# Block 0's two output products in the attention loop: issued whole behind a half-step's scores, or in two column halves around the next step

## The chip, the cores and the metric

One core of one Trainium2 chip runs the kernel. The metric is the device time of one execution in microseconds: 515.57 us before the change, the median of 3 runs (515.53 to 515.69).

## The reference

A layer with post-normalisation on x of 2 x 1024 rows of 512: attention with 8 heads of width 8, then a gated feed-forward part with int4 weights and group scales (1792 wide), each with a residual and a layer norm. Cut to what matters here:

```python
qk = (x @ Wqk_w.T + Wqk_b).reshape(b, n, H, E, 2)          # H = E = 8
v = (x @ Wv_w.T + Wv_b).reshape(b, n, H, E)
scores = jnp.einsum('bhqd,bhkd->bhqk', q, k)
attn = jax.nn.softmax(scores, axis=-1) / 8
out = jnp.einsum('bhsl,bhlv->bhsv', attn, v)               # -> (b, n, 64)
attention = out @ Wo_w.T + Wo_b                            # 64 -> 512
x = layernorm(x + attention)
x = layernorm(x + (silu(x @ Wg.T) * (x @ Wu.T)) @ Wd.T)    # Wg, Wu, Wd dequantised
```

The change touches `out @ Wo_w.T` of the first 512 rows only.

## The kernel before

The 2048 rows are cut into four blocks of 512 queries (NB = 4), and the eight heads into two groups of four. The attention loop has ALL = 64 steps `n`: block by block, group by group, and within a group the eight tiles of 128 keys. A step has two half-steps (`pair` 0 and 1), each with two heads. Steps 0 to 15 are block 0, steps 16 to 31 block 1.

All of it is Bass code in which each engine's program is written out by hand, with semaphores. Per half-step the engines do this:

- TensorE writes the scores of two heads (L1087, two matmuls of 512 columns that share the array by rows), a pair of first-pass matmuls (L1012), and half of the weighted sums of the step before (L1116, `av`, four heads side by side in 256 of the 512 columns).
- ScalarE takes the exponential of both heads' scores in one instruction of 1024 elements (L782, `exps`).
- VectorE takes row maxima of the first pass (L1315), one instruction a matmul. The first pass computes the scores once more ahead of time, so that the maxima of a group of heads are there before the group starts: 256 matmuls (FIRST), two each half-step, into a ring of three banks (RING). TensorE may write a ring bank when the reduction three places earlier is done.

Between these come "turns", which `turns_at(n, pair)` places in the second half-steps: `M`, the transposed maxima of a coming group; `avT` and `attT`, transposes of a group's and of a block's attention; and `wo`, the output product. For block 0, `WO_AT = (3, 4)` puts its two products into steps 19 and 20; blocks 1 and 2 have theirs in the last steps with banks of their own, block 3 behind the loop. A product (in `turn`, L1063) takes 128 columns of `attT` for each of two row tiles and writes two banks of 512 columns, in float32. ScalarE copies both to `wob` (`wo_out`, L810), and GpSimd adds them to x later (L641).

Scores and turns share four PSUM banks in two pairs, in the order in which `in_shared_banks` lists them, each use taking the other pair than the one before. So a use must wait for the use two places earlier to be read:

```python
for n in range(ALL):
    for pair in range(2):
        order += [("scores", n, pair)] + turns_at(n, pair)
...
if pi >= 2:
    wait_shared_read(pe, *shared[shared_index["scores", n, pair] - 2])
```

Around the first product the list reads scores (19,0), scores (19,1), product 0, scores (20,0), scores (20,1), product 1, scores (21,0), and so on: scores (20,0) wait for the exponential of scores (19,1), and scores (20,1) for the copy of product 0. In a step behind a turn (`firsts_ahead`) the first-pass pair of half-step 0 comes ahead of the scores; in all others it comes behind them. TensorE's program for one half-step is the loop behind `for n in range(DRAIN)`, ScalarE's the one around `exps(n, pair)`.

Of the kernel before, what the change touches and what calls it, by code (L numbers as in the profile page):

```python
# [21 lines left out]
P = 128  # L22
# [3 lines left out]
HD = H * E  # L26
# [3 lines left out]
TB = 512  # L30
# [27 lines left out]
def build(nc, x, xT, wqkT, bqk, wvT, bv, woT, bo, gq, gs, uq, us, dq, ds, ds_next, spread, out):  # L58
    ctx = ExitStack()
    with ctx:  # L60
# [42 lines left out]
        wo_s = sb("wo_s", [2 * HD, D], F32)  # L103
# [168 lines left out]
        def turns_at(n, pair):  # L272

            if pair == 0:
                return []
            f, r = divmod(n + 3, KT)
            if r == 0 and f < NB * NG:
                return [("M", f, 0)]
            f, r = divmod(n - 9, KT)
            if r == 0 and 0 <= f < LASTF:  # L280
                return [("avT", f, 0)]
            r = n - STEPS
            if r == 2:
                return [("attT", 0, 0)]
            if r in WO_AT:
                return [("wo", 0, WO_AT.index(r))]
            return []
# [47 lines left out]
        def shared_banks(*use):  # L335
            return 2 * ((shared_index[use] + 1) % 2)

        def wait_shared_read(engine, kind, n, k):

            if kind == "scores":  # L340
                engine.wait_ge(s_exp, 2 * n + k + 1)
            elif kind == "avT":
                engine.wait_ge(s_norm, n + 1)
            else:
                engine.wait_ge(s_read, out_count[kind, n, k])
# [381 lines left out]
        def _(act):  # L727
# [46 lines left out]
            def exps(n, pair):  # L774

                pi, at = 2 * n + pair, shared_banks("scores", n, pair)
                act.wait_ge(s_scf, pi + 1)
                if pi == 0:
                    act.wait_ge(s_row, 5)
                if n >= 2 and pair == 0:  # L780
                    act.wait_ge(s_av, 2 * (n - 1))
                nc.scalar.activation(pbuf[:, pi % 4, :].rearrange("p (a n) -> p a n", a=2), ps[:, at:at + 2, :], ACT.Exp,  # L782
                                     scale=gamma[:, n // (ALL // B):n // (ALL // B) + 1]).then_inc(s_exp, 1)
# [32 lines left out]
            def turn_out(kind, u, k):  # L816
                if kind == "attT":
                    att_out(u)
                if kind == "wo":
                    wo_out(u, k)  # L820
                if kind == "M":
                    max_out(u)
# [24 lines left out]
            for n in range(ALL):  # L847
                for pair in range(2):
                    exps(n, pair)
                    if pair and n and n % KT == 0:  # L850
                        av_out(n // KT - 1)
                    for use in turns_at(n, pair):
                        turn_out(*use)
            nc.scalar.activation(warm[:], mhalf[:, 0:1], ACT.Silu)
            av_out(NB * NG - 1)

# [77 lines left out]
        def _(pe):  # L934
# [85 lines left out]
            def ring_use(kind, n):  # L1020
                i = ring_index[kind, n]
                if i >= 3:

                    wait_ring_read(pe, *ring_order[i - 3])
                if kind == "first":
                    first_pass(n)
                elif kind == "tops":
                    turn_tops(n, ring_bank(kind, n))
                else:
                    turn_maxima(0, ring_bank("M", 0)).then_inc(s_rf, 1)  # L1030

            def turn(kind, u, k):

                if (kind, u, k) in aside:
                    wait_ring_read(pe, "first", FIRST - 1)
                    for other in before_in_bank(kind, u, k):
                        wait_aside_read(pe, other)
                    at = aside_bank(kind, u, k)
                else:
                    i = shared_index[kind, u, k]  # L1040
                    wait_shared_read(pe, *shared[i - 2])
                    at = shared_banks(kind, u, k)
                dst = bank[at]
                if kind == "M":
                    mm = turn_maxima(u, dst)
                elif kind == "avT":

                    pe.wait_ge(s_ave, u + 1)
                    for t in range(BT):
                        mm = nc.tensor.transpose(dst[:, t * P:(t + 1) * P], avt[:, u % 2, t * P:(t + 1) * P], ident[:])  # L1050
                elif kind == "attT":

                    pe.wait_ge(s_norm, NG * (u + 1))
                    for t in range(0, BT, 2):
                        mm = nc.tensor.transpose(dst[:, t * HD:(t + 2) * HD],
                                                 att[:, u, t:t + 2, :].rearrange("p t n -> p (t n)"), ident[:])
                else:
                    if k == 0:
                        pe.wait_ge(s_wo, 16)
                        wait_attT(pe, u)  # L1060
                    for j in range(2):
                        rows = slice(j * HD, (j + 1) * HD)
                        mm = nc.tensor.matmul(bank[at + j], attT[rows, k * P:(k + 1) * P], wo_s[rows, :],  # L1063
                                              start=True, stop=True)
                mm.then_inc(s_of, 1)

            def scores(n, pair):

                u, s = divmod(n, STEPS)
                g, kt = divmod(s, KT)  # L1070
                b, k = divmod(u, N // TB)
                pi = 2 * n + pair
                if kt == 0 and pair == 0:
                    pe.wait_ge(s_mld[g], 16 * 2 * (u + 1))
                at = shared_banks("scores", n, pair)
                if pi >= 2:
                    wait_shared_read(pe, *shared[shared_index["scores", n, pair] - 2])
                elif pi == 0:

                    pe.wait_ge(s_vc, 2 * B)  # L1080
                    pe.wait_ge(s_kept, len(placed) - 1)
                    pe.wait_ge(s_kept1, 1)
                else:
                    pe.wait_ge(s_projr, 6)
                for j in range(2):
                    rows, t = slice(ROWS * j, ROWS * (j + 1)), 2 * g + pair
                    mm = nc.tensor.matmul(bank[at + j], ks[b][rows, t, kt * P:(kt + 1) * P],  # L1087
                                          qs[b][rows, k, t, :], start=True, stop=True)
                mm.then_inc(s_scf, 1)
# [14 lines left out]
            def av(n, half):  # L1104

                u, s = divmod(n, STEPS)
                g, kt = divmod(s, KT)
                b = u * TB // N
                pe.wait_ge(s_exp, 2 * n + 2)
                if n == 0:  # L1110
                    pe.wait_ge(s_vc, 2 * B)
                if kt == 0 and n:
                    pe.wait_ge(s_ave, n // KT)
                lo, hi = half * TB // 2, (half + 1) * TB // 2
                for j in range(HG):
                    mm = nc.tensor.matmul(bank[AVB][j * VC:(j + 1) * VC, lo:hi], vst[b][:, kt, g * HG + j, :],  # L1116
                                          pbuf[:, (2 * n + j // 2) % 4, (j % 2) * TB + lo:(j % 2) * TB + hi],
                                          start=(kt == 0 and half == 0), stop=(kt == KT - 1), skip_group_check=True)
                mm.then_inc(s_av, 1)
# [48 lines left out]
            for n in range(DRAIN):  # L1168
                after_group_start = n % KT == 1
                for pair in range(2):  # L1170
                    firsts_ahead = n and pair == 0 and turns_at(n - 1, 1)
                    if firsts_ahead:
                        for use in ring_uses_at(n, pair):
                            ring_use(*use)
                    scores(n, pair)
                    if after_group_start and pair:
                        av(n - 1, 0)
                    if not firsts_ahead:
                        for use in ring_uses_at(n, pair):
                            ring_use(*use)  # L1180
                    for use in turns_at(n, pair):
                        turn(*use)
                    if n and (pair or not after_group_start):
                        av(n - 1, pair)
            for n in range(DRAIN, ALL):
                scores(n, 0)
                for use in aside_at(n, 1):
                    turn(*use)
                scores(n, 1)
                for use in turns_at(n, 1):  # L1190
                    turn(*use)
                av_whole(n - 1)
# [405 lines left out]
```

## Time and profile before

| | |
|---|---|
| median of 3 runs | 515.57 us |
| the profiled execution | 515.66 us |
| its span, first to last instruction | 513.8 us |
| granted TensorE clock, mean | 0.999 |
| busy, TensorE / VectorE / ScalarE / GpSimd | 499.6 / 410.4 / 405.4 / 258.4 us |
| exponentials, L782 | 128, mean 1114 ns |
| first-pass reductions, L1315 | 256, mean 682 ns |
| copies of products to `wob`, L810 | 4, of 1.02 us |

The profiled execution took 1.9 us more than its span, which is counted from the first to the last instruction. Busy times of TensorE are those of overlapping matmuls: two rows that start 0.23 us apart may each last 0.38 us. Where an instruction group "x4" stands in a row, its time runs from the start of the first to the end of the last. The attention loop of this section ends near 212 us, and the products of block 0 stand at 100.60 and 104.05 us.

### The profile page before, as it was taken

What the parts mean: (1) busy time and instruction counts of PE and PEld (TensorE: products, weight loads), DVE (VectorE), ACT (ScalarE), POOL (GpSimd) and SP (SyncE); (2) the same over time, 40 slices, a digit from 0 to 9 for tenths busy, and PEclk for the clock granted to TensorE, in tenths of its full rate; (3) what the DMA queues carried; (4) which work ended last, traced back from release to release, by engine and by line L of the source; (5) the groups of instructions that cost most, each with busy time, mean ns of one, the idle gap of its engine ahead of it and who ended that gap; (6) DMA issues with size and microseconds to landing.
All of it is one profiled execution on the core that took longest, in us unless ns stands there. A gap on an engine that the chain in (4) does not pass through costs nothing.

```text
span 513.8 us, 8129 instructions
## 1 busy us (share of the span) xinstructions
PE 499.6 (97%) x2986; PEld 194.5 (38%) x2986; DVE 410.4 (80%) x699; ACT 405.4 (79%) x563; POOL 258.4 (50%) x298
## 2 busy tenths in 40 slices
PE   8999999999999999999999999999999999999994
PEld 3222233323333322334444444444444444444441
DVE  2799999999999996478778778778668666788676
ACT  1523889898898889868888888888888888888883
POOL 9200091833101624072664686676885874748741
PEclk9999999999999999999999999999999999999999
DMA  6410017675720007600041121130020020000022
GB/s 194 149 57 13 14 50 206 196 144 108 112 40 2 2 5 142 247 1 0 4 59 20 22 41 22 20 63 1 1 82 1 0 84 0 3 0 1 0 82 82
DMA packets 30151, 29.21 MB, mean 57 GB/s; under 512 B 19488, under 2 KB 21920, under 8 KB 29856
## 3 DMA queue, kind: packets, MB, share of 16 engines
q1 hardware_dynamic: 26544, 22.41, 15.5%
q0 software_dynamic: 3424, 6.03, 6.5%
q8 instruction: 23, 0.38, 0.3%
q10 hardware_dynamic: 144, 0.26, 0.1%
q14 instruction: 16, 0.13, 0.1%
HBM read 24.37 MB, written 4.23 MB: 56 GB/s over the span
## 4 chain that ended last, share of the span: by engine, by line
PE 87%; DVE 7%; ACT 3%; issue 1%; DMA 1%; SPq 0%; POOLq 0%; POOL 0%; DVEq 0%
PE ps L1139 19%; PE ps L1127 19%; PE ps L1218 18%; PE ps L1116 9%; PE ps L1012 7%; PE ps L1087 6%; DVE mxh L1315 4%; PE ps L942 3%; ACT pbuf L782 3%; PE ps L1063 1%; PE ps L1099 1%; DMA arena<-xT 1%; PE ps L994 1%; PE ps L952 1%; PE ps L1050 1%
## 5 line engine op out<-in xcount | busy, mean ns | idle before, releaser
L1315 DVE TENSOR_REDUCE mxh<-ps 128x1 f32<-128x512 f32 x256 | 156.7, 682 | 3.3 <-PE ps L1012 2.4
L782 ACT ACTIVATE pbuf<-ps,gamma 128x1024 f32<-128x1024 f32 x128 | 137.2, 1114 | 16.6 <-PE ps L1087 13.1
L865 ACT ACTIVATE ps<-ps,ratio 128x512 f32<-128x512 f32 x167 | 105.8, 659 | 41.5 <-PE ps L1127 38.6
L1218 PE MATMUL ps<-wd,stack 128*128 128x512 f16 x440 | 129.7, 379 | 0.0
L1139 PE MATMUL ps<-arena,wu 128*128 128x512 f16 x448 | 115.4, 379 | 0.0
L1127 PE MATMUL ps<-arena,wg 128*128 128x512 f16 x448 | 115.3, 379 | 0.1
L1499 DVE TENSOR_TENSOR ps<-ps,stack 128x512 f32<-128x512 f32 x128 | 87.8, 695 | 32.3 <-PE ps L1218 30.3
L871 ACT ACTIVATE ps<-ps,ratio 128x512 f32<-128x512 f32 x156 | 98.9, 659 | 5.6 <-PE ps L1139 1.2
L1499 DVE TENSOR_TENSOR ps<-ps,pbuf 128x512 f32<-128x512 f32 x76 | 52.6, 696 | 23.2 <-PE ps L1218 22.4
L677 POOL CAST stack<-pbuf 128x512 f16<-128x512 f32 x55 | 33.5, 609 | 74.5 <-DVE pbuf L1474 74.5
L1116 PE MATMUL ps<-pbuf,arena 128*32 128x256 f32 x832 | 66.5, 391 | 0.4
L679 POOL TENSOR_TENSOR stack<-pbuf,stack 128x512 f16<-128x512 f32 x55 | 63.6, 1156 | 4.5
L1127 PEld LDWEIGHTS ps<-arena,wg 128*128 128x128 f16 x448 | 43.5, 98 | 54.4 <-issue 1.7
L1139 PEld LDWEIGHTS ps<-arena,wu 128*128 128x128 f16 x448 | 43.4, 98 | 54.2 <-DVE pbuf L1474 2.7
L1218 PEld LDWEIGHTS ps<-wd,stack 128*128 128x128 f16 x440 | 43.0, 98 | 52.1 <-DVE ps L1499 0.4
L1012 PE MATMUL ps<-stack 64*128 64x512 f16 x256 | 61.1, 383 | 1.3 <-DVE mxh L1315 0.7
L1087 PE MATMUL ps<-stack 64*128 64x512 f16 x256 | 50.5, 385 | 0.8 <-ACT pbuf L782 0.5
L573 POOL CAST mp<-mx 128x16 f16<-128x16 f32 x8 | 1.6, 196 | 98.0 <-DVE mx L1325 98.0
L1474 DVE SCALAR_TENSOR_TENSOR pbuf<-ps,scales,pbuf 128x512 f32<-128x512 f32 x56 | 41.9, 748 | 6.3 <-PE ps L1139 6.1
L879 ACT ACTIVATE pbuf<-ps,scales 128x512 f32<-128x512 f32 x56 | 38.1, 680 | 0.2 <-PE ps L1127 0.2
L1012 PEld LDWEIGHTS ps<-stack 64*128 64x128 f16 x256 | 21.1, 93 | 41.5 <-DVE mxh L1315 34.8
L1087 PEld LDWEIGHTS ps<-stack 64*128 64x128 f16 x256 | 12.3, 93 | 47.9 <-issue 30.9
(126 smaller groups left out, 389.4 us busy)
## 6 DMA issues: line engine op xcount, KB each, us to landing
arena<-xT SPq DMA_DIRECT2D x16, 256.0 KB, 5.8
x<-x SPq DMA_DIRECT2D x2, 2048.0 KB, 9.8
out<-x SPq DMA_DIRECT2D x3, 1024.0 KB, 4.2
stack<-down_ratios SPq DMA_DIRECT2D x1, 2048.0 KB, 9.6
wg<-gq POOLq DMA_DIRECT2D x4, 448.0 KB, 7.3
wu<-uq POOLq DMA_DIRECT2D x4, 448.0 KB, 7.2
wd<-dq POOLq DMA_DIRECT2D x2, 896.0 KB, 10.7
pbuf<-down_ratios SPq DMA_DIRECT2D x1, 1536.0 KB, 6.3
```

The costliest lines, as they stand in the source:

```text
L679: nc.gpsimd.tensor_tensor(mparts[:, 1, t % NM, :], sg[t % 2], mparts[:, 0, t % NM, :], ALU.subtract)\
L782: nc.scalar.activation(pbuf[:, pi % 4, :].rearrange("p (a n) -> p a n", a=2), ps[:, at:at + 2, :], ACT.Exp, scale=gamma[:, n // (ALL // B) ...
L865: nc.scalar.activation(gbank[t % 2], gbank[t % 2], ACT.Copy, scale=gr[:, t % G, c:c + 1])\
L871: nc.scalar.activation(ubank[t % 2], ubank[t % 2], ACT.Copy, scale=ur[:, t % G, c:c + 1])\
L1012: nc.tensor.matmul(ring_bank("first", n), qs[b][rows, k, t, qt * P:(qt + 1) * P], ks[b][rows, t, half * TB:(half + 1) * TB], start=True, s ...
L1087: mm = nc.tensor.matmul(bank[at + j], ks[b][rows, t, kt * P:(kt + 1) * P], qs[b][rows, k, t, :], start=True, stop=True)
L1116: mm = nc.tensor.matmul(bank[AVB][j * VC:(j + 1) * VC, lo:hi], vst[b][:, kt, g * HG + j, :], pbuf[:, (2 * n + j // 2) % 4, (j % 2) * TB + ...
L1127: mm = nc.tensor.matmul(gbank[t % 2], wg[:, c, i * P:(i + 1) * P], x1v[blk][:, a, c, :, :], start=(c == 0 and a == 0), stop=(a == 1), skip ...
L1139: mm = nc.tensor.matmul(ubank[t % 2], wu[:, c, i * P:(i + 1) * P], x1v[blk][:, a, c, :, :], start=(c == 0 and a == 0), stop=(a == 1), skip ...
L1218: mm = nc.tensor.matmul(bank[k], mparts[:, a, t % NM, k * P:(k + 1) * P], wd[:, i, :], start=(i == 0 and a == 0), stop=(a == 1), skip_grou ...
L1315: nc.vector.tensor_reduce(mxh[:, f % 2, qh, half:half + 1], ring_bank("first", n), AX.X, ALU.max)\
L1499: nc.vector.tensor_tensor(dst, bank[k], by, ALU.mult).then_inc(s_dr[k], 1)
```

## The change

TensorE: a product of block 0 is no longer a turn in its half-step. `begin_product` computes columns 0 to 255 of both banks behind the half-step's weighted sums; `finish_product` computes columns 256 to 511 in the next step, behind the scores of its half-step 0, and signals the whole product. ScalarE: the copy to `wob` comes behind the next step's first exponential. The list of shared banks, the waits of the scores, and the other turns are as they were.

```diff
             for n in range(ALL):
                 for pair in range(2):
                     exps(n, pair)
+                    if pair == 0 and n:
+                        for use in turns_at(n - 1, 1):
+                            if use[0] == "wo":
+                                turn_out(*use)
                     if pair and n and n % KT == 0:
                         av_out(n // KT - 1)
                     for use in turns_at(n, pair):
-                        turn_out(*use)
+                        if use[0] != "wo":
+                            turn_out(*use)
...
+            def product_half(u, k, half):
+
+                at, cols = shared_banks("wo", u, k), slice(half * TB // 2, (half + 1) * TB // 2)
+                for j in range(2):
+                    rows = slice(j * HD, (j + 1) * HD)
+                    mm = nc.tensor.matmul(bank[at + j][:, cols], attT[rows, k * P:(k + 1) * P], wo_s[rows, cols],
+                                          start=(half == 0), stop=True, skip_group_check=True)
+                return mm
+
+            def begin_product(kind, u, k):
+
+                wait_shared_read(pe, *shared[shared_index[kind, u, k] - 2])
+                if k == 0:
+                    pe.wait_ge(s_wo, 16)
+                    wait_attT(pe, u)
+                product_half(u, k, 0)
+
+            def finish_product(kind, u, k):
+
+                product_half(u, k, 1).then_inc(s_of, 1)
...
                     if not firsts_ahead:
                         for use in ring_uses_at(n, pair):
                             ring_use(*use)
+                    if pair == 0 and n:
+                        for use in turns_at(n - 1, 1):
+                            if use[0] == "wo":
+                                finish_product(*use)
                     for use in turns_at(n, pair):
-                        turn(*use)
+                        if use[0] != "wo":
+                            turn(*use)
                     if n and (pair or not after_group_start):
                         av(n - 1, pair)
+                    for use in turns_at(n, pair):
+                        if use[0] == "wo":
+                            begin_product(*use)
```

TensorE before, from the scores of half-step (19,1) to the weighted sums behind scores (20,0). L1087 are scores, L1012 first-pass matmuls, L1063 the product, L1116 weighted sums; `turn_read_by_act` is a copy of ScalarE's, `exp_done` an exponential.

```order
L1087 MATMUL ps<-stack 128x512 [waits turn_read_by_act]
L1087 MATMUL ps<-stack 128x512
L1012 MATMUL ps<-stack 128x512 [waits first_pass_reduced] x2
L1063 MATMUL ps<-wo_s,attT 128x512 [waits turn_read_by_act,out_weights_loaded,exp_done]
L1063 MATMUL ps<-wo_s,attT 128x512
L1116 MATMUL ps<-pbuf,arena 32x256 [waits exp_done]
L1116 MATMUL ps<-pbuf,arena 32x256 x3
L1012 MATMUL ps<-stack 128x512 [waits first_pass_reduced] x2
L1087 MATMUL ps<-stack 128x512 [waits exp_done]
L1087 MATMUL ps<-stack 128x512
L1116 MATMUL ps<-pbuf,arena 32x256 [waits exp_done]
L1116 MATMUL ps<-pbuf,arena 32x256 x3
```

The same place with the change, from the first pass of (19,1) to the first matmul of scores (20,1) (L1113 scores, L1017 first pass, L1077 product halves, L1142 weighted sums):

```order
L1017 MATMUL ps<-stack 128x512 [waits first_pass_reduced] x2
L1142 MATMUL ps<-pbuf,arena 32x256 [waits exp_done]
L1142 MATMUL ps<-pbuf,arena 32x256 x3
L1077 MATMUL ps<-wo_s,attT 128x256 [waits turn_read_by_act,out_weights_loaded,exp_done]
L1077 MATMUL ps<-wo_s,attT 128x256
L1017 MATMUL ps<-stack 128x512 [waits first_pass_reduced] x2
L1113 MATMUL ps<-stack 128x512 [waits exp_done]
L1113 MATMUL ps<-stack 128x512
L1077 MATMUL ps<-wo_s,attT 128x256 x2
L1142 MATMUL ps<-pbuf,arena 32x256 [waits exp_done]
L1142 MATMUL ps<-pbuf,arena 32x256 x3
L1113 MATMUL ps<-stack 128x512 [waits turn_read_by_act]
```

The weighted sums have moved ahead of the product, and its second half stands behind the scores of (20,0). The scores of (20,1) wait for ScalarE's copy of the product, as they did before.

ScalarE from the exponentials of step 18 to the turn of the maxima in step 21; the difference, with L782 the exponentials, L814 the copy to `attT`, L810 the copy to `wob` and L803 that of the maxima:

```order
 L814 ACTIVATE attT<-ps 128x256
-L782 ACTIVATE pbuf<-ps,gamma 128x1024 x2
+L782 ACTIVATE pbuf<-ps,gamma 128x1024 x3
 L810 ACTIVATE wob<-ps 128x1024
 L782 ACTIVATE pbuf<-ps,gamma 128x1024 x2
 L810 ACTIVATE wob<-ps 128x1024
-L782 ACTIVATE pbuf<-ps,gamma 128x1024 x2
+L782 ACTIVATE pbuf<-ps,gamma 128x1024
 L803 ACTIVATE mrows<-ps 48x128
```

Each of the two copies has one more exponential ahead of it.

## Rows read from the trace of the kernel before

**Rows 1.** Page, part 1: busy us (share of the span) x instructions, by engine.
```profile
PE 499.6 (97%) x2986; PEld 194.5 (38%) x2986; DVE 410.4 (80%) x699; ACT 405.4 (79%) x563; POOL 258.4 (50%) x298
```

**Rows 2.** Windows: us, busy PE, PEld, DVE, ACT, POOL, granted clock, DMA share, GB/s.
```profile
99.30:106.20 6.90, 6.70 (x58) 1.77 (x56) 5.25 (x10) 6.23 (x6) 2.32 (x7) 1.00 0.94 176
112.00:124.00 12.00, 11.93 (x124) 3.81 (x121) 11.97 (x22) 10.77 (x12) 6.71 (x8) 1.00 0.81 154
```

**Rows 3.** VectorE in order of time: start us, us, engine line op, xcount [idle before <-releaser].
```profile
96.65 5.17 DVE L1315 TENSOR_REDUCE mxh<-ps 128x1 f32<-128x512 f32 x8
102.66 1.29 DVE L1315 TENSOR_REDUCE mxh<-ps 128x1 f32<-128x512 f32 x2 [0.83 <-PE ps L1012]
...
104.08 1.28 DVE L1315 TENSOR_REDUCE mxh<-ps 128x1 f32<-128x512 f32 x2
106.10 12.42 DVE L1315 TENSOR_REDUCE mxh<-ps 128x1 f32<-128x512 f32 x20 [0.75 <-PE ps L1012]
...
125.12 13.36 DVE L1315 TENSOR_REDUCE mxh<-ps 128x1 f32<-128x512 f32 x22
```

**Rows 4.** Groups of VectorE by line, from 106.1 to 184.9 us.
```profile
L1315 DVE TENSOR_REDUCE mxh<-ps 128x1 f32<-128x512 f32 x126 | 76.6, 682 | 0.9 <-PE ps L1012 0.7
```

**Rows 5.** Chain of waits at the loop's end: start us, us, what.
```profile
184.91 0.18 DVE mx L1325
```

**Rows 6.** ScalarE in order of time, from 99.4 to 112 us.
```profile
99.44 2.12 ACT L782 ACTIVATE pbuf<-ps,gamma 128x1024 f32<-128x1024 f32 x2 [0.37 <-PE ps L1087]
101.78 1.02 ACT L810 ACTIVATE wob<-ps 128x1024 f32<-128x1024 f32 x1 [0.23 <-PE ps L1063]
102.88 2.12 ACT L782 ACTIVATE pbuf<-ps,gamma 128x1024 f32<-128x1024 f32 x2
105.22 1.02 ACT L810 ACTIVATE wob<-ps 128x1024 f32<-128x1024 f32 x1 [0.23 <-PE ps L1063]
106.33 2.12 ACT L782 ACTIVATE pbuf<-ps,gamma 128x1024 f32<-128x1024 f32 x2
108.34 0.26 ACT L803 ACTIVATE mrows<-ps 48x128 f16<-48x128 f16 x1
108.93 3.12 ACT L782 ACTIVATE pbuf<-ps,gamma 128x1024 f32<-128x1024 f32 x3 [0.34 <-PE ps L1087]
```

**Rows 7.** TensorE in order of time, from 100 to 110 us.
```profile
100.12 0.38 PE L1012 MATMUL ps<-stack 64*128 64x512 f16 x2
100.60 1.13 PE L1063 MATMUL ps<-wo_s,attT 64*128 64x512 f32 x4
101.66 0.64 PE L1116 MATMUL ps<-pbuf,arena 128*32 128x256 f32 x8
102.23 0.39 PE L1012 MATMUL ps<-stack 64*128 64x512 f16 x2
102.46 0.38 PE L1087 MATMUL ps<-stack 64*128 64x512 f16 x2
...
103.34 0.39 PE L1087 MATMUL ps<-stack 64*128 64x512 f16 x2
...
109.62 0.38 PE L1012 MATMUL ps<-stack 64*128 64x512 f16 x2
109.93 0.64 PE L1116 MATMUL ps<-pbuf,arena 128*32 128x256 f32 x8
```

**Rows 8.** TensorE in the last steps of the loop, and the window of its stand.
```profile
192.53 1.04 PE L1063 MATMUL ps<-wo_s,attT 64*128 64x512 f32 x4
193.38 0.40 PE L1087 MATMUL ps<-stack 64*128 64x512 f16 x2
...
195.81 0.63 PE L1050 MATMUL ps<-ident,avt 128*128 128x128 f32 x4 [0.71 <-ACT avt L789]
...
194.00:197.00 3.00, 2.29 (x20) 0.77 (x16) 2.90 (x4) 2.87 (x5) 2.84 (x4) 1.00 0.51 96
```

**Rows 9.** Instructions on `wob`: GpSimd's additions.
```profile
L641 POOL TENSOR_TENSOR x<-wob,x x8: 1262/1276/1309, 113.7 to 223.0; 128x512 f32<-128x512 f32 x8
```

## The prediction

> **What bounds the kernel now.** I read the page first, then the stretch around the change by windows, then the three engines there in order of time, then the chain of waits. The page [rows 1] shows TensorE busy for 97% of the span, VectorE 80% and ScalarE 79%: an average over stages that says little about the one stage touched. The windows [rows 2] say more. From 112 to 124 us, an ordinary piece of the loop, VectorE is busy 11.97 of 12.00 us and ScalarE 10.77. From 99.3 to 106.2 us, where block 0's two output products stand, VectorE drops to 5.25 of 6.90. So the loop runs at VectorE's pace, one reduction of the first pass after another, except here. That pace is 22 reductions in 13.36 us [rows 3], 0.60 from one start to the next and 1.21 a half-step.
>
> VectorE in order of time [rows 3] shows what the products cost it: 0.83 us idle before 102.66 and 0.75 before 106.10, both ended by first-pass matmuls, 1.58 us in all. Behind that it has no slack that could swallow a shift: from 106.1 to 184.9 us its 126 reductions have 0.9 us idle before them in all, 0.7 of it the stall just named [rows 4]. At the loop's end the chain of waits passes from VectorE's last reductions and combine at 184.91 straight into the last steps [rows 5]. Time lost or won on VectorE by 106 us is therefore lost or won at the end.
>
> ScalarE [rows 6] is the other half. It takes two exponentials of 1.11 us a step (a pair is 2.12 and three are 3.12, so each further one starts 1.01 or 1.00 later) and, in the two steps of the change, also the copy of the product to `wob`, 1.02 us. The exponentials that matter start at 99.44 and 100.45 (19,0 and 19,1), 102.88 and 103.89 (20,0 and 20,1), 106.33 and 107.34 (21,0 and 21,1), 108.93 (22,0). The copies stand between steps, at 101.78 and 105.22. While a copy runs, TensorE makes the next step's first scores.
>
> **What the change moves.** Nothing is added to the arithmetic: two full products of two matmuls become four halves of two matmuls each. TensorE's order: the second half-step's weighted sums no longer stand behind a whole product, and the second half of the product comes behind scores (20,0) and (21,0). ScalarE's order: the copy comes behind exponential (20,0) or (21,0). What decides is the rotation of the two bank pairs, which isn't changed: scores (n, pair) may be written when the use two places earlier has been read. For scores (20,0) that is exponential (19,1), for scores (20,1) it is the copy of the product. That copy now comes a whole exponential later, and behind scores (20,1) on TensorE stand first-pass matmuls (20,1), for which VectorE waits.
>
> **The sum**, from the start of exponential (19,1) at 100.45 us. Steps on TensorE [rows 7], start to start: weighted sums 0.57 (101.66 to 102.23); first-pass pair to scores 0.23 (102.23 to 102.46); scores to first-pass pair, as many columns, 0.23 too; first-pass pair to weighted sums 0.31 (109.62 to 109.93). Scores start to exponential start is 0.42 (102.46 to 102.88); first-pass start to VectorE's reduction 0.43 (102.23 to 102.66). The end of an exponential frees TensorE 0.05 us later (99.44 + 1.11 = 100.55, product at 100.60 [rows 6, 7]).
> No row shows a half product. The nearest: a full one took 1.06 us where TensorE had stood idle before it (100.60 to 101.66) and 0.85 where it came straight behind scores (192.53 to 193.38) [rows 7, 8]. The new halves come straight behind other work, so I take half of 0.85, 0.43; the bounds are 0.43 and, if the width did not count, 1.06.
> (a) First-pass pair (19,1) at 100.12, weighted sums 100.43, half product 101.00, first-pass pair (20,0) 101.43, scores (20,0) 101.66. Exponential (19,1) ended at 101.56, so it doesn't hold them. First-pass results reach VectorE at 101.86, and it is free at 101.82 [rows 3]: its idle 0.83 is gone, as the change would have it. Exponential (20,0) starts at 102.08, 0.80 earlier than before.
> (b) The product's second half is issued at 101.89 and is done long before ScalarE is free. The copy starts 1.00 behind the exponential's start (as the copy at 108.34 behind 107.34 [rows 6]), at 103.08, and ends at 104.10. Only then scores (20,1), at 104.15; before they stood at 103.34. Exponential (20,1) starts at 104.57: 0.68 late. TensorE has by then issued the second half (0.43) and weighted sums (19,0) (0.57, and 0.08 for the change from one to the other, which is what 0.31 has over 0.23) by 102.97 and stands for 1.2 us. First-pass pair (20,1) goes at 104.38 and reaches VectorE at 104.81 against 104.08: 0.73 late, with more than a microsecond idle before it.
> (c) Weighted sums at 104.69, half product 105.26, first-pass pair (21,0) 105.69, scores (21,0) 105.92: reduction at 106.12, exponential (21,0) at 106.34, both level with before (106.10, 106.33). The faster half gives back what (b) lost.
> (d) Copy from 107.34 to 108.36, scores (21,1) at 108.41, exponential at 108.83 against 107.34: 1.49 late. There is no third product to win it back.
> (e) Exponential (21,1) ends at 109.94 and frees the pair for scores (22,0); exponential (22,0) comes at 110.42 against 108.93. The shift stays 1.49, and behind it VectorE sets the pace again.
> By steps: (a) −0.80, (b) +1.48, (c) −0.67, (d) +1.48; together **+1.5 us**. The profiled execution took 515.66, so 517.2; against the median of 515.57, 517.1. With a half product of 1.06 (a) and (c) each grow by 0.63, 518.4. Were TensorE's work in (a) and (c) shorter than I have it, the ends of the exponentials would set the start of the scores, 0.05 and 0.19 us earlier: 516.9.
>
> What I cost at nothing: the four more matmuls are the halves of the sum above; the copies are 1.3 and 2.1 us later, but GpSimd's additions of `wob` begin only at 113.7 [rows 9], 5 us behind the later one; the turn of the maxima behind scores (21,1) shifts with the rest and keeps its distance to the step that needs it.
>
> **Rivals.** *The banks come free in time (faster).* If the copy did not hold scores (20,1) and (21,1), both of VectorE's stalls would vanish and nothing come instead: 1.58 us less, 514.0. For it: the first stall goes, (a). The point that decides is when the copy has ended: TensorE reaches scores (20,1) at about 103.0, so the copy would have to start by 102.0, when the exponential ahead of it can only just start (scores at 101.6, and 0.42). Only a mistake of mine about who holds those banks would save it. Chance 0.08.
> *Made good on the way (no change).* The late step could meet work that was waiting anyway: first-pass results stored in the three ring banks, or a step behind (22,0) where ScalarE has 1.23 us to spare in 12 [rows 2]. If all of (d) were made good the level of (c) would stay, 515.6; if half of it, 516.3. For it: ScalarE has that spare time. Against: the loop isn't ScalarE's; VectorE is dry in (b) and (d) for longer than three banks last, and has nothing idle to give later [rows 4]. Chance 0.15.
> *The clock falls.* TensorE would now stand twice for 1.2 us, and with it short gaps at each PSUM rotation. A stand of 0.71 us before 195.81 left the granted clock at 1.00 [rows 8]. Were the clock to fall to the lower of its two levels, 1.2 of 2.4 GHz, TensorE's 1.11 us of a half-step (0.57 + 0.23 + 0.31) would double and pass VectorE's 1.21 by 1.0 us; three such half-steps give 3 us on top of the sum, 520.1. The Trainium skill's page "TensorE: Matmul & The Clock Gate", section "A second HAM failure mode: psum-queue depth-cycling", warns of just this, micro-idles between matmul groups while PSUM banks are cycled; by that rule the change would be worse than my sum. The stand of 0.71 speaks against it so far. Chance 0.03.
>
> **How the numbers follow.** The forecast has 0.74, its rivals 0.08, 0.15 and 0.03. The likeliest time is 517.1. A measurement of this kernel can tell about 0.2% from no change, 1.03 us, so 516.6 begins slower: the sum's lower bound, 516.9, lies just above it. The range reaches from 516.0, the upper part of the case made good, to 518.4, a half product that costs as much as a whole one. Faster 0.08, within 0.2% 0.17 (the case made good and a little of the forecast), slower 0.75.
>
> **What would show it.** VectorE's idle before 102.66 gone, but two stalls of over 1 us new, before the reductions of (20,1) and (21,1), near 104.8 and 109.1. ScalarE's copies near 103.1 and 107.3, each with an exponential right before it and an idle 0.4 to 0.5 behind it. TensorE's scores (20,1) and (21,1) released by the copy, L810. From 112 us on everything as before, 1.5 us later, and the clock at 1.00. The forecast is wrong if those scores start without waiting for the copy, or if the distance to the old trace at 125 us is not the one at the end.

## The result, and the profile after

The changed kernel takes 517.07 us (median of 7 runs, 516.67 to 517.55) against 515.53 (median of 7, 515.15 to 515.69): ratio 1.0028, 95% interval 1.0018 to 1.0038, which is 0.9 to 2.0 us slower. The forecast was 517.1 in a range of 516.0 to 518.4.

Windows of the changed kernel, in the order of [rows 2]: us, then busy time of TensorE, its weight loads, VectorE, ScalarE, GpSimd; granted clock; DMA share; GB/s.

```profile
99.30:106.20 6.90, 5.78 (x60) 2.60 (x56) 5.14 (x10) 5.06 (x6) 2.47 (x8) 1.00 0.92 169
112.00:124.00 12.00, 11.93 (x124) 3.84 (x121) 11.97 (x22) 10.86 (x12) 7.13 (x8) 1.00 0.81 154
```

Around the products TensorE, ScalarE and VectorE have all lost busy time: TensorE 6.70 to 5.78, ScalarE 6.23 to 5.06, VectorE 5.25 to 5.14. When none of the three is busier and it takes longer, they wait for each other. From 112 to 124 us VectorE is busy 11.97 of 12.00 us as before, and the clock is at 1.00.

ScalarE of the changed kernel in order of time, answering to [rows 6] (L782 exponentials, L810 copies of products, L803 that of the maxima):

```profile
98.99 2.12 ACT L782 ACTIVATE pbuf<-ps,gamma 128x1024 f32<-128x1024 f32 x2 [0.36 <-PE ps L1113]
101.72 1.11 ACT L782 ACTIVATE pbuf<-ps,gamma 128x1024 f32<-128x1024 f32 x1 [0.62 <-PE ps L1113]
102.73 1.02 ACT L810 ACTIVATE wob<-ps 128x1024 f32<-128x1024 f32 x1
104.24 1.11 ACT L782 ACTIVATE pbuf<-ps,gamma 128x1024 f32<-128x1024 f32 x1 [0.49 <-PE ps L1113]
106.08 1.11 ACT L782 ACTIVATE pbuf<-ps,gamma 128x1024 f32<-128x1024 f32 x1 [0.73 <-PE ps L1113]
107.09 1.02 ACT L810 ACTIVATE wob<-ps 128x1024 f32<-128x1024 f32 x1
108.60 1.11 ACT L782 ACTIVATE pbuf<-ps,gamma 128x1024 f32<-128x1024 f32 x1 [0.49 <-PE ps L1113]
109.61 0.26 ACT L803 ACTIVATE mrows<-ps 48x128 f16<-48x128 f16 x1
110.20 3.12 ACT L782 ACTIVATE pbuf<-ps,gamma 128x1024 f32<-128x1024 f32 x3 [0.33 <-PE ps L1113]
```

ScalarE's two waits of 0.23 us for the products have gone, and four between exponentials have come: 0.62 and 0.73 ahead of the copy's exponential, 0.49 behind each copy, all ended by scores (L1113).

TensorE of the changed kernel in the same steps, answering to [rows 7] (L1142 weighted sums, L1077 product halves, L1017 first pass, L1113 scores):

```profile
99.98 0.64 PE L1142 MATMUL ps<-pbuf,arena 128*32 128x256 f32 x8
100.55 0.70 PE L1077 MATMUL ps<-wo_s,attT 64*128 64x256 f32 x4
101.08 0.38 PE L1017 MATMUL ps<-stack 64*128 64x512 f16 x2
101.30 0.38 PE L1113 MATMUL ps<-stack 64*128 64x512 f16 x2
101.52 0.60 PE L1077 MATMUL ps<-wo_s,attT 64*128 64x256 f32 x4
102.05 0.64 PE L1142 MATMUL ps<-pbuf,arena 128*32 128x256 f32 x8
103.81 0.39 PE L1113 MATMUL ps<-stack 64*128 64x512 f16 x2 [1.12 <-ACT wob L810]
104.03 0.38 PE L1017 MATMUL ps<-stack 64*128 64x512 f16 x2
...
108.17 0.39 PE L1113 MATMUL ps<-stack 64*128 64x512 f16 x2 [1.12 <-ACT wob L810]
```

Ahead of scores (20,1) at 103.81 and (21,1) at 108.17 TensorE stands idle for 1.12 us, waiting for the copy. VectorE shows the same from its side (answering to [rows 3]; L1349 reductions, L1359 the combine):

```profile
97.40 5.39 DVE L1349 TENSOR_REDUCE mxh<-ps 128x1 f32<-128x512 f32 x8
102.82 0.18 DVE L1359 TENSOR_TENSOR mx<-mxh 128x16 f32<-128x16 f32 x1
104.44 2.70 DVE L1349 TENSOR_REDUCE mxh<-ps 128x1 f32<-128x512 f32 x4 [1.45 <-PE ps L1017]
108.80 4.38 DVE L1349 TENSOR_REDUCE mxh<-ps 128x1 f32<-128x512 f32 x7 [1.66 <-PE ps L1017]
...
186.18 0.18 DVE L1359 TENSOR_TENSOR mx<-mxh 128x16 f32<-128x16 f32 x1
```

The old stalls of 0.83 and 0.75 are gone from the rows (about 0.14 us of the first is left, before the reduction that starts at 101.50), and 1.45 and 1.66 have come half a step later each. The last combine, with which the loop's last steps begin, is at 186.18 against 184.91 [rows 5].

**A ruler that doesn't move with the start.** The changed kernel's trace reaches the exponential (19,0) 0.45 us earlier than before, at 98.99 against 99.44, though nothing ahead of it was changed. The lag is there when the loop begins: its first exponentials, before the change and behind it,

```profile
50.33 4.12 ACT L782 ACTIVATE pbuf<-ps,gamma 128x1024 f32<-128x1024 f32 x4
```

```profile
49.89 4.12 ACT L782 ACTIVATE pbuf<-ps,gamma 128x1024 f32<-128x1024 f32 x4
```

and it comes from the first projections, which wait for the loads of x: they end at 13.07 us here and at 13.49 before. In the traces of this study, the loop's first exponential lies between 49.70 and 52.30 us. So for what the products cost I take the distance from exponential (19,0) to the last combine of the first pass: 184.91 − 99.44 = 85.47 before, 186.18 − 98.99 = 87.19 after, **+1.72 us**. In the tables this is "distance". The runs' +1.54 has the start's scatter in it; its interval holds both.

### The profile page after: what moved, and what is told of

Its sections match the earlier page's. It is cut to its first block, busy times and chain, and to the rows that moved or that the text cites. A ratio compares the mean times of both kernels' runs of the same rounds, so it can differ in the third digit from the quotient of the medians.

```text
span 515.1 us, 8145 instructions
## 1 busy us (share of the span) xinstructions
PE 499.5 (97%) x2994; PEld 195.7 (38%) x2994; DVE 410.5 (80%) x699; ACT 405.5 (79%) x563; POOL 258.4 (50%) x298
## 4 chain that ended last, share of the span: by engine, by line
PE 87%; DVE 7%; ACT 3%; issue 1%; DMA 1%; POOLq 0%; SPq 0%; POOL 0%; DVEq 0%
PE ps L1165 19%; PE ps L1153 19%; PE ps L1252 18%; PE ps L1142 9%; PE ps L1017 7%; PE ps L1113 6%; DVE mxh L1349 4%; PE ps L947 3%; ACT pbuf L782 2%; PE ps L1125 1%; PE ps L999 1%; PE ps L957 1%; DMA arena<-xT 1%; PE ps L1068 1%; PE ps L1055 1%
## 5 line engine op out<-in xcount | busy, mean ns | idle before, releaser
L1349 DVE TENSOR_REDUCE mxh<-ps 128x1 f32<-128x512 f32 x256 | 156.7, 682 | 4.9 <-PE ps L1017 4.0
L782 ACT ACTIVATE pbuf<-ps,gamma 128x1024 f32<-128x1024 f32 x128 | 137.4, 1114 | 18.7 <-PE ps L1113 15.4
L1142 PE MATMUL ps<-pbuf,arena 128*32 128x256 f32 x832 | 66.5, 391 | 0.4
L1017 PE MATMUL ps<-stack 64*128 64x512 f16 x256 | 61.1, 382 | 1.3 <-DVE mxh L1349 0.6
L1113 PE MATMUL ps<-stack 64*128 64x512 f16 x256 | 50.6, 384 | 3.0 <-ACT wob L810 2.2
L1017 PEld LDWEIGHTS ps<-stack 64*128 64x128 f16 x256 | 21.2, 93 | 40.8 <-DVE mxh L1349 33.6
L1113 PEld LDWEIGHTS ps<-stack 64*128 64x128 f16 x256 | 12.3, 92 | 50.5 <-issue 30.5
```

The source lines that it names most:

```text
L1017: nc.tensor.matmul(ring_bank("first", n), qs[b][rows, k, t, qt * P:(qt + 1) * P], ks[b][rows, t, half * TB:(half + 1) * TB], start=True, s ...
L1349: nc.vector.tensor_reduce(mxh[:, f % 2, qh, half:half + 1], ring_bank("first", n), AX.X, ALU.max)\
```

## The experiments

Each was timed beside the kernel before on the same chip (medians 515.61, 515.66 and 515.64 in the three sets), with an interval of about ±0.4 to 0.6 us; the distance comes from one profiled execution of each.

| kernel | median, us | ratio (interval) | distance | against before |
|---|---|---|---|---|
| before | 515.6 | | 85.47 | |
| changed | 517.07 | 1.0028 (1.0018 to 1.0038) | 87.19 | +1.72 |
| copy late, product as before | 518.05 | 1.0047 (1.0035 to 1.0059) | 88.21 | +2.74 |
| whole product behind the sums | 515.76 | 1.0004 (0.9996 to 1.0013) | 85.56 | +0.09 |
| halves, copy ahead of the exponential | 516.71 | 1.0018 (1.0010 to 1.0027) | 86.61 | +1.14 |
| changed, copy of one bank | 516.07 | 1.0014 (1.0006 to 1.0022) | 86.30 | +0.83 |
| before, copy of one bank | 515.75 | 0.9999 (0.9991 to 1.0008) | 85.46 | −0.01 |
| changed for product 0 alone | 516.05 | 1.0008 (0.9999 to 1.0017) | 86.02 | +0.55 |
| before, second product in step 22 | 515.36 | 0.9998 (0.9989 to 1.0007) | 85.46 | −0.01 |
| whole behind the sums, copy shared | 515.81 | 1.0003 (0.9993 to 1.0012) | 85.31 | −0.16 |
| before, copy shared | 515.82 | 1.0004 (0.9995 to 1.0013) | 85.47 | 0.00 |

**1. The late copy alone.** ScalarE as in the change, TensorE as before.

```diff
                     exps(n, pair)
+                    if pair == 0 and n:
+                        for use in turns_at(n - 1, 1):
+                            if use[0] == "wo":
+                                turn_out(*use)
...
                     for use in turns_at(n, pair):
-                        turn_out(*use)
+                        if use[0] != "wo":
+                            turn_out(*use)
```

> The kernel before, with ScalarE's copies of block 0's products moved behind the next step's first exponential and TensorE's order left alone. Theory (the late copy holds the bank pair that scores (20,1) and (21,1) need): each product costs about 1.6 us and nothing is won back, +3.2 us, 518.7. Rival (the halves on TensorE cost the time, not the copy's place): no change, 515.5.

Measured +2.74 in distance and 2.4 us by medians: without a single half product the kernel is slower than with both parts of the change. The theory stands, the rival falls; the size was 0.5 us too large. TensorE of this kernel (L1092 scores, L1068 products, L1121 weighted sums) shows a part of why. First the kernel before around its second product (L1012 first pass, L1063 product, L1116 weighted sums), then this run at the same place:

```profile
103.57 0.38 PE L1012 MATMUL ps<-stack 64*128 64x512 f16 x2
104.05 1.13 PE L1063 MATMUL ps<-wo_s,attT 64*128 64x512 f32 x4
105.11 0.64 PE L1116 MATMUL ps<-pbuf,arena 128*32 128x256 f32 x8
```

```profile
104.34 0.39 PE L1092 MATMUL ps<-stack 64*128 64x512 f16 x2 [1.56 <-ACT wob L810]
104.57 0.38 PE L1017 MATMUL ps<-stack 64*128 64x512 f16 x2
104.78 1.02 PE L1068 MATMUL ps<-wo_s,attT 64*128 64x512 f32 x4
105.74 0.64 PE L1121 MATMUL ps<-pbuf,arena 128*32 128x256 f32 x8
```

Before, the product came 0.48 behind its first-pass pair, since it waited for exponential (20,0), and took 1.06; here that exponential has long ended, and it comes 0.21 behind and takes 0.96. The wait for the copy gives back a wait for an exponential. I had left that out. It is worth 0.26 us at exponential (21,0), which starts 2.18 behind (20,1) here (104.78 to 106.96) and 2.44 before (103.89 to 106.33 [rows 6]). The rest of the 0.5 is that each late copy cost 1.5 us and not 1.6.

**2. Only TensorE's order.** The product whole, behind the weighted sums; copies as before.

```diff
                     for use in turns_at(n, pair):
-                        turn(*use)
+                        if use[0] != "wo":
+                            turn(*use)
                     if n and (pair or not after_group_start):
                         av(n - 1, pair)
+                    for use in turns_at(n, pair):
+                        if use[0] == "wo":
+                            turn(*use)
```

> The kernel before, with the products still whole but behind the half-step's weighted sums; copies where they were. Theory: the product ends about 0.35 us later, and with it copy and next exponential: +0.3 us for each or for both together, 515.8 to 516.2. Rival (moving the product behind the weighted sums is the costly part): +1.5 us, 517.0.

Measured +0.09 in distance, 0.15 by medians: less than the +0.3 expected, and the rival falls. In this trace the copy starts 0.40 us later than before, counted from exponential (19,0), but exponential (20,0) only 0.22 and (22,0) only 0.13: most of the delay is won back within three steps. The order of product and weighted sums is worth next to nothing either way.

**3. Halves, but the copy first.** The changed kernel with ScalarE's loop of before, so that the copy waits for the second half.

> The changed kernel, with the copies back ahead of the next step's first exponential, so that ScalarE waits for the second half of the product. Theory: scores (20,1) and (21,1) come 0.5 to 0.9 us earlier than in the changed kernel, exponentials (20,0) and (21,0) later; about 0.5 us less than the changed kernel, 516.6. Rival (halves cost the time): same as the changed kernel, 517.1.

Measured 0.58 less in distance than the changed kernel (+1.14), 0.4 less by medians (+1.10 for +1.54). ScalarE of this kernel:

```profile
99.25 2.12 ACT L782 ACTIVATE pbuf<-ps,gamma 128x1024 f32<-128x1024 f32 x2 [0.36 <-PE ps L1108]
102.43 1.02 ACT L810 ACTIVATE wob<-ps 128x1024 f32<-128x1024 f32 x1 [1.06 <-PE ps L1072]
103.35 2.11 ACT L782 ACTIVATE pbuf<-ps,gamma 128x1024 f32<-128x1024 f32 x2
106.39 1.02 ACT L810 ACTIVATE wob<-ps 128x1024 f32<-128x1024 f32 x1 [0.93 <-PE ps L1072]
107.31 2.11 ACT L782 ACTIVATE pbuf<-ps,gamma 128x1024 f32<-128x1024 f32 x2
```

ScalarE now stands 1.06 and 0.93 us for the product. What its second half stands behind is shown by TensorE (L1072 product halves, L1012 first pass, L1108 scores):

```profile
100.82 0.70 PE L1072 MATMUL ps<-wo_s,attT 64*128 64x256 f32 x4
101.35 0.38 PE L1012 MATMUL ps<-stack 64*128 64x512 f16 x2
101.57 0.38 PE L1108 MATMUL ps<-stack 64*128 64x512 f16 x2
101.78 0.60 PE L1072 MATMUL ps<-wo_s,attT 64*128 64x256 f32 x4
...
105.15 0.38 PE L1012 MATMUL ps<-stack 64*128 64x512 f16 x2
105.52 0.39 PE L1108 MATMUL ps<-stack 64*128 64x512 f16 x2
105.74 0.59 PE L1072 MATMUL ps<-wo_s,attT 64*128 64x256 f32 x4
```

For product 0 these four follow each other without a wait: the second half is late because a first-pass pair and the scores stand between the halves. For product 1 the scores also wait 0.15 us for exponential (20,1), 0.37 behind the first-pass pair instead of 0.22. So the split has a price of its own: with the product finished behind the next scores, the copy is late whichever place it has on ScalarE, and its place behind the exponential makes it later.

The three steps add up to the change: the product behind the weighted sums +0.09 (experiment 2), the split with the copy still first 1.05 more (+1.14 here), the copy's late place 0.58 more (+1.72). What the split is worth depends on the copy's place: with the copy first it costs 1.05, and once the copy is late, split and order together save 1.02 (2.74 in experiment 1, 1.72 in the changed kernel).

**4 and 5. A shorter copy, after and before.** Both kernels, with block 0's copies taking only the product's first bank: 0.59 us instead of 1.02. The second bank's results are left out and the first's are added twice.

```diff
-                nc.gpsimd.tensor_tensor(x1[:, n, :], wob[:, t, :], x1[:, n, :], ALU.add).then_inc(s_add, 1)
+                nc.gpsimd.tensor_tensor(x1[:, n, :], wob[:, t if u else t // 2 * 2, :], x1[:, n, :], ALU.add).then_inc(s_add, 1)
...
-                nc.scalar.activation(wob[:, 2 * k:2 * k + 2, :], ps[:, at:at + 2, :], ACT.Copy).then_inc(s_read, 1)
+                n = 2 if u else 1
+                nc.scalar.activation(wob[:, 2 * k:2 * k + n, :], ps[:, at:at + n, :], ACT.Copy).then_inc(s_read, 1)
```

> The changed kernel, but the two copies of block 0 take only the first bank of each product (its second bank is left out, and GpSimd adds the first twice). A copy is then 0.59 us instead of 1.02. Theory: the copy is on the path twice, so 2 x 0.43 = 0.86 us less than the changed kernel, 516.2. Rival (halves): same as the changed kernel, 517.1.

> The kernel before, with the same short copies of block 0 (one bank of two; the second bank's product left out). Theory: here the copy runs beside TensorE's weighted sums and next scores and is not on the path: at most 0.1 us each, 515.3 to 515.5. Rival (ScalarE's own work is the bound in these steps, wherever the copy stands): 0.86 us less, 514.7.

Measured in distance: from the changed kernel 87.19 − 86.30 = 0.89 less (1.08 by medians, +0.46 for +1.54), from the kernel before 0.01. Both rivals fall. The same 0.43 us counts in full, twice, where the copy stands behind the exponential, and not at all where it stands ahead of it. ScalarE of the changed kernel with the short copy, and then of the kernel before with it:

```profile
104.11 1.11 ACT L782 ACTIVATE pbuf<-ps,gamma 128x1024 f32<-128x1024 f32 x1 [0.62 <-PE ps L1114]
105.12 0.59 ACT L811 ACTIVATE wob<-ps 128x512 f32<-128x512 f32 x1
106.20 1.11 ACT L782 ACTIVATE pbuf<-ps,gamma 128x1024 f32<-128x1024 f32 x1 [0.49 <-PE ps L1114]
```

```profile
101.20 0.60 ACT L811 ACTIVATE wob<-ps 128x512 f32<-128x512 f32 x1 [0.23 <-PE ps L1064]
102.30 2.12 ACT L782 ACTIVATE pbuf<-ps,gamma 128x1024 f32<-128x1024 f32 x2 [0.51 <-PE ps L1088]
```

In the first the next exponential starts 1.08 behind the copy's start, where it was 1.51, with the same 0.49 idle: the copy is on the path. In the second it starts 1.10 behind, as before (101.78 to 102.88 [rows 6]): what the copy no longer takes has become idle time, 0.51, ended by scores. The 3.44 us from exponential (19,0) to (20,0) of the kernel before are a chain without the copy: the exponential 1.11, then 0.05 to the product, product 1.06, weighted sums 0.57, first-pass pair 0.23, and 0.42 from the scores to the next exponential [rows 6, 7].

**6. Product 0 alone.** The changed kernel, with `if use == ("wo", 0, 0)` where the diff has `if use[0] == "wo"`.

> The changed kernel with the change for product 0 alone; product 1 and its copy as before. Theory: terms (a) and (b) give +0.8 us at exponential (20,1), and the whole product 1 behind it gives back about 0.2: +0.6 us, 516.1; the second product is then worth 1.0 us. Rival (each product costs the same): half of the change, +0.8 us, 516.3; rival (only a shift of the start, not the products): +1.5 us or 0.

Measured +0.55 in distance; the second product brings the other 1.17. That is the order of my steps: a whole product 1 behind the first change still wins a little back (exponential (20,1) is 0.80 late, (21,0) 0.54), behind the second nothing does. By medians (+0.4, interval −0.1 to +0.9) the two rivals of +0.8 and 0 would both pass; the distance tells them apart.

**7. The products further apart.** The kernel before with `WO_AT = (3, 6)`.

> The kernel before, with the second product in step 22 instead of 20 (WO_AT = (3, 6)), to see whether two products in a row cost more than two apart. Theory: each product costs VectorE its own stall of 0.75 to 0.83 us, so no change within 0.2 us, 515.5. Rival (ScalarE's backlog of one product delays the next): up to 0.5 us faster, 515.0.

Measured −0.01 in distance: two products in a row cost no more than two apart, and ScalarE carries no backlog from one to the next. The medians (−0.3, interval −0.6 to +0.4) would not tell the theory from the rival's 0.5.

**8 and 9. A version meant to beat both.** Experiment 2, and as its control the kernel before, with the copy shared: ScalarE takes one bank, VectorE the other. The lines show VectorE's part; ScalarE's is that of experiments 4 and 5, and whoever waited for the copy now waits for both parts.

```diff
                     for kind, f, k in turns_at(n, pair):
                         if kind == "avT":
                             normalise(f)
+                        if kind == "wo":
+                            dve.wait_ge(s_of, turn_count[kind, f, k])
+                            nc.vector.tensor_copy(wob[:, 2 * k + 1, :], bank[shared_banks(kind, f, k) + 1]).then_inc(s_half2, 1)
```

> A version meant to beat both: the whole product behind the weighted sums, and its copy shared, one bank by ScalarE and one by VectorE in its stall behind the half-step's reductions. Theory (in these steps the path runs from exponential (19,0) over product, weighted sums, first pass and scores to exponential (20,0), with ScalarE's two exponentials and copy just as long beside it; both must be shortened): from exponential (19,0) to the loop's end 0.4 us less than before, 515.2. Rival (VectorE has no time for a copy of 0.65 us, since the loop runs at its pace): 0.3 to 1.3 us slower than before.

> Control to the one above: the kernel before with the shared copy alone, the product where it was. Theory: TensorE's own order is the path, the shorter copy brings nothing and VectorE's part fits into its stall of 0.8 us: 0.0 to 0.1 us, 515.6. Rival (VectorE's pace): 1.3 us slower.

Measured −0.16 and 0.00 in distance, and by medians no difference from before in either. In distance the direction held, the size did not: 0.16 for the 0.4 expected. Both rivals, 0.3 to 1.3 us slower, fall by the distance. VectorE of the first:

```profile
97.80 3.38 DVE L1325 TENSOR_REDUCE mxh<-ps 128x1 f32<-128x512 f32 x5
101.53 0.69 DVE L1450 COPY wob<-ps 128x512 f32<-128x512 f32 x1 [0.35 <-PE ps L1069]
102.14 1.28 DVE L1325 TENSOR_REDUCE mxh<-ps 128x1 f32<-128x512 f32 x2
...
104.94 0.69 DVE L1450 COPY wob<-ps 128x512 f32<-128x512 f32 x1
105.55 6.76 DVE L1325 TENSOR_REDUCE mxh<-ps 128x1 f32<-128x512 f32 x11
```

VectorE stands 0.35 us in all and then runs through: its own pace is the bound again, with two copies of 0.6 us in it. That is why so little is left to win: two copies 0.61 us long, start to next start, and the 0.35 make 1.57 us, for the 1.58 of the two old stalls. Whether something other than a copy could fill them at a gain, no run here shows. No version here is faster than the kernel before by an amount that its runs can tell.

## Why the prediction was right

Distances from the start of exponential (19,0), forecast and measured in the changed kernel's trace:

| exponential | before | forecast | measured |
|---|---|---|---|
| (20,0) | 3.44 | 2.64 | 2.73 |
| (20,1) | 4.45 | 5.13 | 5.25 |
| (21,0) | 6.89 | 6.90 | 7.09 |
| (21,1) | 7.90 | 9.39 | 9.61 |
| (22,0) | 9.49 | 10.98 | 11.21 |

- **(a)** held: the first stall of VectorE vanished, and exponential (20,0) came 0.71 earlier for the 0.80 forecast. The step was mis-sized by 0.09, by the price of a half product: 0.43 was taken, and both measure 0.53 (100.55 to 101.08, 101.52 to 102.05). The row that I halved, 0.85, stands between scores on both sides. A whole product with weighted sums on one side of it took 0.96 without any idle ahead (experiment 1, 104.78 to 105.74; experiment 2, 101.87 to 102.83), 0.11 more; the first half had 0.10 over its 0.43. For the second half I had charged 0.08 for this neighbour, so it was nearly right; for the first half I had charged nothing. What the 0.1 us consists of, no run here separates. The upper bound of 1.06 was far too wide.
- **(b) and (d)** held to 0.03 each: copy 1.01 behind the exponential's start, 1.02 long, then scores 0.06 later and the exponential 0.43 behind them. Experiments 4 and 5 show that the copy is on this path and was on none before; experiment 1 that its place alone costs more than the whole change.
- **(c)** won back 0.60 (from +0.80 to +0.20) for the forecast 0.67, the half product again.
- **(e)** held: the shift is 1.72 at exponential (22,0), 1.71 at the combine near 125 us and 1.72 at the last one, for the forecast 1.49. The 0.23 are 0.09 of (a), 0.07 of (c) and 0.03 each of (b) and (d). In the medians it is +1.54.
- **The bounds** 516.9 and 518.4 were added to the profiled execution's 517.2, the forecast of 517.1 to the median; against the median they are 516.8 and 518.3.
- **The rivals.** The banks did not come free in time: scores (20,1) and (21,1) are released by L810, 1.12 us each. Nothing was made good on the way. The granted clock stayed at 1.00 through two stands of 1.12 us, so the rule of the Trainium skill's page "TensorE: Matmul & The Clock Gate", section "A second HAM failure mode: psum-queue depth-cycling", did not come into play; two stands of 1.56 us in experiment 1 left it at 1.00 from 98 to 112 us as well. So the three slow half-steps and the 3 us with which I priced that rival have nothing in these traces behind them.
- **What was left out**: that a late copy also frees the second product of its wait for an exponential. In the changed kernel the weighted sums ahead of the product already cover that wait, so nothing was lost by it there; it was the error of experiment 1's expectation.

The exact agreement of 517.07 with 517.1 is partly luck: in distance the sum was 0.23 us under, and the medians, with the start's scatter in them, show 0.18 less than the distance.

## What to carry to other kernels

When an operation's result sits in a buffer that rotates, moving its reader later moves every use that stands two places behind it, and all that is queued behind that use; write down who holds the buffer before you fill a stall. Two stalls that look like the fault of a long instruction may be the shortest form of a ring of waits: shorten one member alone first (here the copy, by 0.43 us) and see whether the ring shrinks. For effects of a few tenths of a per cent, measure between two instructions of the trace that lie around the change, not from the start of the execution.

## What the runs showed that I had not expected

The body of this kernel repeats to a few hundredths of a microsecond from one execution to another: in the four kernels whose middle wasn't slowed or sped up (before, and before with a short copy, with a shared copy, and with the second product in step 22) the distances are 85.47, 85.46, 85.47 and 85.46. From the loop's first exponential to (19,0) it is 49.1 us in all eleven traces, and from the last combine to the end of the span 328.9 or 329.0. So the spans differ in the first 20 us, where the projections wait for the loads of x; the loop's first exponential lay anywhere from 49.70 to 52.30 us. A second scatter lies outside the span: the executions took 1.8 to 3.0 us more than theirs. The first projections (L942) of the kernel before, all but the two that start at 5.20 us, and of the latest of the eleven, the changed kernel with the short copy, where they stand at L948:

```profile
7.21 6.28 PE L942 MATMUL ps<-arena,wqk_s 128*128 128x512 f32 x14 [0.91 <-DMA arena<-xT]
```

```profile
6.48 8.99 PE L948 MATMUL ps<-arena,wqk_s 128*128 128x512 f32 x16 [0.85 <-DMA arena<-xT]
```

They end at 13.49 us in the one and at 15.47 in the other, 1.98 later, and the loop begins 1.97 later (52.30 against 50.33). A float32 product of 256 columns in two row tiles takes 0.53 us from its start to the next group's, more than half of the 0.85 that 512 columns took between scores.
